# Perceiver block on one core: the expert blocks' first two products as three rounded-format products each

## What is computed

```python
y = rmsnorm(x, rms_w)                                  # D = 256
logits = einsum('bsd,ed->bse', y, gate_w)              # 8 experts, the best 2 per token
vals, idx = top_k(logits, 2);  w = softmax(vals)
up   = einsum('bsd,end->bsen', y, W1)                  # 704 hidden values per expert
gate = einsum('bsd,end->bsen', y, W2)
h    = silu(up) * gate
out  = einsum('bsen,emn->bsem', h, W3)
return x + sum over the chosen experts of w * out
```

## Time and profile before

| | |
|---|---|
| median of 3 runs | 3649.42 us (3645.97 to 3651.94) |
| profiled execution: its own time | 3645.97 us |
| profiled execution: span of the core | 3644.1 us |
| stage of the expert blocks | 1231 to 1581 us of the span |
| first product of block 0 to the last `m_out` | 1239.57 to 1577.88 us |
| mean granted clock | 0.955 of full speed |

### The profile page before, as it was taken

How to read it: one execution, slowest core, us unless ns; L and a number is a source line. 1 busy time by engine, 2 the same in 40 slices (tenths; PEclk the granted TensorE clock), 3 DMA queues, 4 the chain that set the end, 5 groups by cost and what they waited for, 6 DMA issues and landing times. The chain is left out here.

```text
span 3644.1 us, 131527 instructions
## 1 busy us (share of the span) xinstructions
PE 3298.8 (91%) x56442; PEld 2668.9 (73%) x56443; DVE 2498.4 (69%) x4351; ACT 2188.0 (60%) x3459; POOL 1487.7 (41%) x1421
## 2 busy tenths in 40 slices
PE   9999999999887499979999999999885888888779
PEld 6888888888777366647888888888634666666667
DVE  5777777777545122237767777777659999999976
ACT  5666666666553122225766666666657888888743
POOL 4433333333122300035333333333007899999930
PEclk9999999999987699979999999999988999999999
DMA  2000000010003411011100000010001111111110
GB/s 83 31 31 31 31 31 31 31 37 25 12 2 145 167 32 32 29 70 48 38 30 31 31 30 31 31 39 13 28 9 41 44 47 47 46 46 47 47 34 24
DMA packets 61319, 148.37 MB, mean 41 GB/s; under 512 B 8963, under 2 KB 29187, under 8 KB 60515
## 3 DMA queue, kind: packets, MB, share of 16 engines
q1 hardware_dynamic: 57154, 130.78, 11.0%
q0 software_dynamic: 3072, 8.39, 0.7%
q10 hardware_dynamic: 544, 1.05, 0.1%
HBM read 123.42 MB, written 16.78 MB: 38 GB/s over the span
## 5 line engine op out<-in xcount | busy, mean ns | idle before, releaser
L799 ACT ACTIVATE x_probs<-x_score_ps 128x1024 f32<-128x1024 f32 (+1 forms) x896 | 814.2, 961 | 646.1 <-PE x_score_ps L625 618.7
L904 DVE TENSOR_REDUCE x_maxes<-x_misc_ps 128x1 f32<-128x512 f32 (+1 forms) x1792 | 1022.5, 627 | 34.8 <-PE x_misc_ps L543 30.1
L836 POOL CAST x_kT_hi<-x_kT 128x512 fp32r<-128x512 f32 (+1 forms) x448 | 253.5, 566 | 1168.6 <-ACT x_kT L702 1082.0
L2453 POOL TENSOR_TENSOR b_drive<-b_b_all,b_dtx 128x1024 f32<-128x1024 f32 x256 | 601.7, 2368 | 244.9 <-DVE b_dtx L2547 176.0
L2510 DVE TENSOR_TENSOR_SCAN b_state<-b_decay_ps,b_drive 128x512 f32<-128x512 f32 x512 | 598.8, 1211 | 34.5 <-POOL b_drive L2453 25.9
L619 PE MATMUL x_score_ps<-x_qz,x_kT 32*128 32x128 f32 x13312 | 592.4, 278 | 1.1 <-issue 0.7
L619 PEld LDWEIGHTS x_score_ps<-x_qz,x_kT 32*128 32x128 f32 x13312 | 502.1, 182 | 5.5 <-issue 3.0
L590 PE MATMUL x_misc_ps<-x_probs,x_v 128*32 128x64 f32 x26624 | 466.1, 221 | 1.2 <-issue 0.9
L590 PEld LDWEIGHTS x_misc_ps<-x_probs,x_v 128*32 128x32 f32 x26624 | 393.3, 110 | 79.7 <-issue 39.8
L2277 PE MATMUL b_turn_ps<-ident,b_state 128*128 128x128 f32 x2048 | 299.0, 288 | 153.9 <-DVE b_state L2510 97.3
L543 PE MATMUL x_misc_ps<-x_kT_hi,x_qz_hi 32*128 32x512 f32 (+1 forms) x2048 | 429.0, 405 | 8.3 <-ACT x_kT L702 3.2
(11 more groups left out here) (320 smaller groups left out, 5747.6 us busy)
## 6 DMA issues: line engine op xcount, KB each, us to landing
x_raw<-in_ctxT SPq DMA_DIRECT2D x64, 800.5 KB, 4.4
b_b_all<-b_b_rows SPq DMA_DIRECT2D x128, 256.0 KB, 3.3
m_w<-in_m_w SPq DMA_DIRECT2D x16, 704.0 KB
m_w<-in_m_w SPq DMA_DIRECT2D x8, 768.0 KB
m_slot_rows<-m_zero SPq DMA_DIRECT2D x1, 4992.0 KB, 17.6
m_block_rows<-m_slot_rows SPq DMA_DIRECT2D x39, 128.0 KB, 2.1
m_slot_out<-m_out SPq DMA_DIRECT2D x39, 128.0 KB, 1.7
x<-in_x SPq DMA_DIRECT2D x4, 512.0 KB, 6.8
```

The lines of the kernel that those rows point to most:

```text
L799: nc.scalar.activation(probs[rows, s % 2, js, 0:n], score_ps[rows, js, 0:n], ACT.Exp).then_inc(exp_done, 1)
L904: nc.vector.tensor_reduce(maxes[:, c:c + m, j, k0 // NB], bank(op)[:, 0:m * even].rearrange("p (c k) -> p c k", c=m)[:, :, 0:kn], AX.X, AL ...
L2453: nc.gpsimd.tensor_tensor(drive[:, h % 3, :, :], b_all[:, k % 2:k % 2 + 1, :].broadcast_to([P, 2, NB]), dtx[:, half * 2:half * 2 + 2, :], ...
```

## The change

The inputs of the first two products are split. ACT rounds the turned rows to `float32r` (`m_y_hi`), DVE computes the rest (`m_y_lo`, from PSUM with the RMS weight again, minus the high part). The block's expert weights are split anew for each block, a quarter (2 x 352 columns, 128x704 in a row) at a time: ACT rounds it from `m_w1` or `m_w2` into `m_w_hi` (`round_quarters`), DVE subtracts into `m_w_lo` (`rest_of_quarters`). Both read the block's expert into a register themselves, twice a step. PE makes each old matmul as three: high by high, high by low, low by high, 24 for a block, each now one instruction on tiles of fixed address; it reads the expert only for W3. `w_used` counts quarters multiplied: ACT may round quarter g of block n+2 when P of block n+1 has used it, and Silu waits for the fourth.

In step n ACT and DVE prepare quarters 0 to 2 of block n+2 before Silu and `m_h` of block n+1, and quarter 3 after them, and DVE also makes `m_y_lo` there. For block 0 all four quarters are split before PE's first product, for block 1 three before the first Silu.

```diff
--- before.py
+++ after.py
@@ -1667,7 +1667,10 @@
     sb, ps, sem = alloc(nc, ctx)
     HN = DE // 2
     rows = sb("m_block_rows", [P, 2, D])
-    yT = sb("m_yT", [P, 2, KD, P])
+    y_hi = sb("m_y_hi", [P, 2, KD, P], F32R)
+    y_lo = sb("m_y_lo", [P, 2, KD, P], F32R)
+    w_hi = sb("m_w_hi", [P, 4, KD, HN], F32R)
+    w_lo = sb("m_w_lo", [P, 4, KD, HN], F32R)
     gate = sb("m_gate", [P, 2, HN])
     h = sb("m_h", [P, 2, HN])
     hT = sb("m_hT", [P, EC, P])
@@ -1679,8 +1682,11 @@
     out_ps = ps("m_out_ps", [P, NB])
     rows_in = [sem(f"m_rows_in{j}") for j in range(2)]
     rows_turned = sem("m_rows_turned")
+    y_hi_done = sem("m_y_hi_done")
     yT_done = sem("m_yT_done")
-    up_done = sem("m_up_done")
+    w_hi_done = sem("m_w_hi_done")
+    w_lo_done = sem("m_w_lo_done")
+    w_used = sem("m_w_used")
     gate_done = sem("m_gate_done")
     h_done = sem("m_h_done")
     h_turned = sem("m_h_turned")
@@ -1704,6 +1710,13 @@
         for b in range(2 * LOOPED, SLOT_BLOCKS):
             step(b // 2, b % 2, b)
 
+    def expert(engine, n):
+        return engine.value_load(block_expert[0:1, ds(n, 1)], min_val=0, max_val=NE - 1)
+
+    def quarter(g, e):
+
+        return (w1, w2)[g // 2][:, ds(e, 1), :, g % 2 * HN:(g % 2 + 1) * HN].rearrange("p e k n -> p (e k) n")
+
     def exists(b, ahead):
         return b is None or b + ahead <= LAST
 
@@ -1741,17 +1754,16 @@
 
         def products(pair, j):
             n = pair * 2 + j
-            e = pe.value_load(block_expert[0:1, ds(n, 1)], min_val=0, max_val=NE - 1)
             pe.wait_ge(yT_done, n + 1)
             pe.wait_ge(h_done, n)
-            for dst, w in ((up_ps, w1), (mul_ps, w2)):
-                for half in range(2):
-                    for k in range(KD):
-                        ins = nc.tensor.matmul(
-                            dst[:, half, 0:HN], yT[:, j, k, :],
-                            w[:, ds(e, 1), k, half * HN:(half + 1) * HN].rearrange("p e n -> p (e n)"),
-                            start=k == 0, stop=k == KD - 1)
-            ins.then_inc(up_done, 1)
+            for g in range(4):
+                pe.wait_ge(w_lo_done, n * 4 + g + 1)
+                dst = (up_ps, mul_ps)[g // 2]
+                for k in range(KD):
+                    for m, (y, w) in enumerate(((y_hi, w_hi), (y_hi, w_lo), (y_lo, w_hi))):
+                        ins = nc.tensor.matmul(dst[:, g % 2, 0:HN], y[:, j, k, :], w[:, g, k, :], start=k == 0 and m == 0,
+                                               stop=k == KD - 1 and m == 2)
+                ins.then_inc(w_used, 1)
 
         def step(pair, j, b):
             n = pair * 2 + j
@@ -1790,11 +1802,18 @@
         def take_rows(n, j):
             act.wait_ge(rows_turned, n + 1)
             for c in range(KD):
-                ins = nc.scalar.activation(yT[:, j, c, :], yT_ps[:, c * P:(c + 1) * P], ACT.Copy, scale=rms_w[:, c:c + 1])
-            ins.then_inc(yT_done, 1)
+                ins = nc.scalar.activation(y_hi[:, j, c, :], yT_ps[:, c * P:(c + 1) * P], ACT.Copy, scale=rms_w[:, c:c + 1])
+            ins.then_inc(y_hi_done, 1)
+
+        def round_quarters(n, of, free):
+            e = expert(act, n)
+            for g in of:
+                if free:
+                    act.wait_ge(w_used, n * 4 - 4 + g + 1)
+                nc.scalar.activation(w_hi[:, g, :, :], quarter(g, e), ACT.Copy).then_inc(w_hi_done, 1)
 
         def silu(n):
-            act.wait_ge(up_done, n + 1)
+            act.wait_ge(w_used, n * 4 + 4)
             act.wait_ge(h_done, n)
             nc.scalar.activation(gate[:, :, :], up_ps[:, :, 0:HN], ACT.Silu).then_inc(gate_done, 1)
 
@@ -1804,18 +1823,39 @@
             act.wait_ge(out_made, n)
             nc.scalar.activation(hT[:, 0:CB, :].rearrange("p c n -> p (c n)"), hT_ps[:, 0, :], ACT.Copy
                                  ).then_inc(hT_done, 1)
+            if exists(b, 2):
+                round_quarters(n + 2, range(3), True)
             if exists(b, 1):
                 silu(n + 1)
             if exists(b, 2):
                 take_rows(n + 2, j)
+                round_quarters(n + 2, range(3, 4), True)
 
         take_rows(0, 0)
+        act.wait_ge(w_in, 16 * 3 * NE)
+        round_quarters(0, range(4), False)
         take_rows(1, 1)
+        round_quarters(1, range(3), True)
         silu(0)
+        round_quarters(1, range(3, 4), True)
         steps(act, step)
 
     @block.vector
     def _(dve):
+        def keep_rest(n, j):
+            dve.wait_ge(y_hi_done, n + 1)
+            for c in range(KD):
+                ins = nc.vector.scalar_tensor_tensor(y_lo[:, j, c, :], yT_ps[:, c * P:(c + 1) * P], rms_w[:, c:c + 1],
+                                                     y_hi[:, j, c, :].bitcast(F32), ALU.mult, ALU.subtract)
+            ins.then_inc(yT_done, 1)
+
+        def rest_of_quarters(n, of):
+            e = expert(dve, n)
+            for g in of:
+                dve.wait_ge(w_hi_done, n * 4 + g + 1)
+                nc.vector.tensor_tensor(w_lo[:, g, :, :], quarter(g, e), w_hi[:, g, :, :].bitcast(F32), ALU.subtract
+                                        ).then_inc(w_lo_done, 1)
+
         def hidden(n):
             dve.wait_ge(gate_done, n + 1)
             dve.wait_ge(h_turned, n * 2)
@@ -1827,14 +1867,24 @@
             dve.wait_ge(out_made, n)
             nc.vector.tensor_copy(hT[:, CB, :], hT_ps[:, 1, 0:P])
             nc.vector.tensor_copy(hT[0:ELAST, CB + 1, :], hT_ps[0:ELAST, 1, P:2 * P]).then_inc(hT_done, 1)
+            if exists(b, 2):
+                rest_of_quarters(n + 2, range(3))
             if exists(b, 1):
                 hidden(n + 1)
+            if exists(b, 2):
+                keep_rest(n + 2, j)
+                rest_of_quarters(n + 2, range(3, 4))
             dve.wait_ge(out_made, n + 1)
             if b is None or b > 1:
                 dve.wait_ge(stored[j], pair * 16)
             nc.vector.tensor_copy(out[:, j, :], out_ps[:, 0:D]).then_inc(out_done, 1)
 
+        keep_rest(0, 0)
+        rest_of_quarters(0, range(4))
+        keep_rest(1, 1)
+        rest_of_quarters(1, range(3))
         hidden(0)
+        rest_of_quarters(1, range(3, 4))
         steps(dve, step)
```

## The result

The changed kernel takes 3626.46 us (median of four runs, 3619.35 to 3626.63) against 3650.68 for the kernel before in the same comparison: ratio 0.993, interval 0.9913 to 0.9947, so 24 us or 0.7% faster. The forecast was 3618 in a range of 3607 to 3634; of its narrower range for the author's own case, 3612 to 3625, the median lies 1.5 us outside. The profiled execution took 3626.63 us, with a span of 3624.5.

What follows compares the result with a forecast made beforehand. PE was taken to bound the kernel: 38 blocks x 0.89 us saved is 33.8, less 2.8 at the start, 31.0; from the median 3649.42 this gives 3618.4 us, with eight in ten between 3607 and 3634.

Steps and rivals of the forecast that it cites:

- the author's own case: Whole kernel: PE stays the bound and the time is 3618 us, range 3612 to 3625; chance 0.70.
- PE bounds the stage, before and after: Steady part of the stage: PE is busy 100.00 of a hundred us and stays the bound with blocks of 7.65 us.
- Products at 0.160, 0.89 saved a block: PE's 24 products of 352 columns: 0.160 us each from a line between 256 and 512 columns, 3.84 instead of 4.73.
- A: PE's products: weight loads set the spacing at 0.190 us, kernel at 3646; chance 0.05.
- E: PE's products: rounded format needs more than one pass at 352 columns, over 85 us slower; chance 0.01 with A's turns.
- D: PE's products: spacing of 0.147 to 0.150 us, kernel at 3608.5; chance 0.08.
- ACT 0.78 a rounding, DVE 0.89 a subtraction, 0.6 for the low rows: Splitting per block: ACT has 5.1 us of work and DVE 6.1 in 7.65, so it fits.
- Register loads, 0.3 each open: ACT and DVE, two loads each per block: 0.6 us a block open, putting DVE at 6.7 of 7.65.
- Rival C: DVE's stream: a register load above 1.2 us makes blocks longer than now; at 1.5, kernel at 3673; chance 0.04.
- B: DVE's splitting becomes the bound if register loads hide behind nothing: block 7.9 us, kernel at 3629; chance 0.12.
- What is late next is nothing; PE stays the bound.: Steady blocks: splitting arrives in time, and the chain to `m_h` keeps its 1.1 us ahead of PE.
- The start costs 2.8, T(0) 2.1 later: Stage's start: PE's first turning of h comes 2.1 us later, plus 0.7 for a fallen clock after the gap.

Runs made afterwards that it cites:

- E2: Two-pass f32 products from the unsplit weights, all splitting kept, against the changed kernel: 3652.59 us, ratio 1.0003.
- E3: Weights split for block 0 alone and used for every block, against the changed kernel: 3617.52 us, ratio 0.9908.
- E5: PE's register load for the output product moved ahead of turning the next rows, against the changed kernel: 3618.48 us, ratio 0.9921.
- E6: SP issues each block's row load one step earlier, against the changed kernel: 3621.98 us, ratio 0.9931.
- E8: Register load first, rows loaded early and a warm start together, against the changed kernel: 3614.36 us, ratio 0.9909.
- E9: DVE's register loads in the splitting made three times, against E8: 3616.24 us, ratio 0.9916.
- E11: The changed kernel measured again without edit, beside E12 on one chip: 3621.9 us, ratio 0.9934.
- E1: The changed kernel measured again, no edit: 3617.83 us, ratio 0.9911.
- E4: Third product (low rows by high weights) left out, against the changed kernel: 3611.32 us, ratio 0.9901.
- E12: E8 measured again without further edit, beside E11 on one chip: 3609.57 us, ratio 0.9895.

## Why the prediction was right, and where it was not

- **PE bounds the stage, before and after.** Right: PE 100.00 at clock 1.00 in both windows, and E2 and E3 show that adding or removing the splitting moves nothing in the steady part.
- **Products at 0.160, 0.89 saved a block.** Right, and a little low: without the disturbance a block is 7.621 (E5, E6), so 0.920 was saved, 24 products at 0.159. The straight line between the rows for 256 and 512 columns held. Rivals A and E fall; so does D, whose best spacing was 0.150. The Trainium skill (page "TensorE: Matmul & The Clock Gate", section "The mechanism") says that a weight load overlaps matmuls in flight only if it goes to other rows of the array. The trace does not agree at 352 columns either: loads of 0.19 us for all 128 rows pass by every 0.16.
- **ACT 0.78 a rounding, DVE 0.89 a subtraction, 0.6 for the low rows.** 0.795, 0.890 and 0.60. Right.
- **Register loads, 0.3 each open.** Right in that they don't bind, too high in what is open: in the steady part they show no idle time with "issue" ahead of the subtractions. With nothing beside them they cost 0.57 to 0.77 on DVE (E8, E9). Rival C needed over 1.2 us and falls; B needed them all in the open.
- **"What is late next is nothing; PE stays the bound."** This step failed, at a small price. The due times were worked out for ACT and DVE only; SP's queue and PE's own sequencer were left out. The row load goes out after the store of the block before, and when the products became shorter its landing came past the point where PE's sequencer had to pass it and make a register load. Cost: 0.088 us a block (7.709 against 7.621), 3.3 us in 37 blocks; by the two other traces of the changed kernel 0.07.
- **The start costs 2.8, T(0) 2.1 later.** Mis-sized. T(0) came 3.96 later (2.86 in E11's trace), since most of block 0's products ran at the lower level of the clock, where the prediction had put the fall behind them; that also held ACT back, whose next roundings wait for PE to have used each quarter (brackets of 0.86 and 0.97), and so pushed the table load and the Silu. In the forecast's own account, where block 1's shorter products are a gain of 0.89 beside the start, the start cost 2.7 + 0.9 = 3.6.
- **Sum.** 31.0 forecast, 28.1 in the stage: 37 x (0.832 - 0.89) = -2.1 and -0.8 at the start. Two misses in the -2.1 partly offset each other, and that is luck: the products saved 0.03 a block more than forecast (+1.1), the late rows took 0.088 (-3.3). The recorded medians differ by 24.2, those of E1's and E11's comparisons by 34 and 25, 28 in the mean. What a single comparison differs from the stage's 28.1 is put down to the scatter of layers that the change doesn't touch; this is argued, not shown.

## What to carry to other kernels

When the bounding engine gets faster, work out due times for every queue that feeds it, DMA issues and the sequencer's own register loads too: a stage at 100% can hide a wait that eats most of the next saving (E4: only 0.17 of 1.27 us came). A register load belongs ahead of a wait, not behind it. Splitting operands on idle engines is free only while their due times hold, and a pipeline's first block, which nothing covers, is worth an order of its own.

## What the runs showed of the hardware

- Products in the rounded format of 352 columns go by every 0.159 us at full clock (0.160 in E9 and E12) and every 0.293 at the lower level; in two-pass form they take 0.296 at full clock.
- PE reported 100.00 busy in the changed kernel's window while the weight loads of its output product came 0.13 us late in the long block shown: short gaps of this kind are covered by the listed ends of the instructions in front. Only the spacing of starts told.
- The clock level in which the stage starts is not the kernel's alone. PE had been idle for 1.45 and then 1.31 us ahead of block 0's products in all of the following. About twenty of the 24 ran at the lower level in the changed kernel and in E1 (T(0) at 13.12 and 13.14 after R), about ten in E5, E6 and E11 (11.93 to 12.06), and none in E3, without any warm-up work. What decides it was not tried.
